# First layer of a four-block transformer step: one norm chain at the end of the feed-forward, the routing's places one key tile later, and VectorE's side work in other portions

## The reference

```python
x = x + attn_a(layernorm(x))   # linear attention: 16 heads of 64, 64 random features, norm, elu feed-forward (512), norm
x = x + ffn(layernorm(x))      # 160 experts, the best 8 by sigmoid score, and a shared expert
x = x + attn_b(layernorm(x))   # softmax attention, causal within 256 tokens
x = x + ffn(layernorm(x))
```

```python
kv = einsum('bnhm,bnhd->bhmd', kf, v); num = einsum('bnhm,bhmd->bnhd', qf, kv)
den = einsum('bnhm,bhm->bnh', qf, sum(kf, axis=1)); attn_out = einsum('bnhd,hdo->bno', num / den, Wo)
out1 = norm(x + attn_out, ln1); h = elu(out1 @ W1 + b1)
return norm(out1 + h @ W2 + b2, ln2)
```

## Time and profile before

| | |
|---|---|
| median of three runs | 2445.37 us |
| profiled execution | 2448.35 us, of which 2445.9 us span |
| TensorE busy | 1809.1 us, 74% |
| VectorE busy | 1664.6 us, 68% |
| GpSimd busy | 1276.6 us, 52% |
| ScalarE busy | 1139.9 us, 47% |
| granted TensorE clock, mean | 0.83 |
| stages 1, 2, 3 with the feed-forward behind them | about 200 to 810 us of the span |

### The profile page before, as it was taken

The page is one execution under the profiler, slowest core; times in us unless marked ns, Lnnn a source line. Parts: engine busy times, 40 slices in busy tenths (PEclk is TensorE's granted clock), DMA queues, the critical chain, the costliest instruction groups (busy, mean ns, idle before and its releaser), DMA issues. The chain is left out here.

```text
span 2445.9 us, 45027 instructions
## 1 busy us (share of the span) xinstructions
PE 1809.1 (74%) x15531; PEld 1047.1 (43%) x15531; DVE 1664.6 (68%) x4684; ACT 1139.9 (47%) x2101; POOL 1276.6 (52%) x1244
## 2 busy tenths in 40 slices
PE   8997787787687678774989888988899868874000
PEld 4555455445445455551334343443344346653000
DVE  8477578588678664576888878888887266376222
ACT  4663553454544356651548554534453536653000
POOL 0162166667756675763436430531342477577776
PEclk9998898789789689995789887988886879987555
DMA  9940101201203687875133221212211378775222
GB/s 358 343 190 30 44 3 57 78 6 43 80 20 143 234 272 246 268 242 129 44 88 78 53 77 36 61 62 47 60 61 42 137 280 285 252 246 183 60 61 55
DMA packets 143465, 309.20 MB, mean 126 GB/s; under 512 B 30668, under 2 KB 45644, under 8 KB 137340
## 3 DMA queue, kind: packets, MB, share of 16 engines
q1 hardware_dynamic: 110472, 239.16, 29.3%
q0 software_dynamic: 32768, 67.17, 9.3%
HBM read 163.12 MB, written 142.70 MB: 125 GB/s over the span
## 5 line engine op out<-in xcount | busy, mean ns | idle before, releaser
L1523 POOL DMA_INDIRECT slots_in<-g_xs,g_place x512 | 519.1, 1014 | 307.5 <-ACT b_pT L2614 155.1
L2614 ACT ACTIVATE b_pT<-b_psE 128x512 f32<-128x512 f32 (+3 forms) x768 | 331.9, 492 | 383.6 <-PE b_psE L2515 206.9
L1550 POOL DMA_INDIRECT r_xs<-slots_out,g_place x336 | 328.1, 976 | 230.2 <-issue 86.0
L2366 DVE TENSOR_REDUCE b_peak<-b_psM 128x1 f32<-128x512 f32 (+3 forms) x768 | 388.9, 549 | 82.8 <-PE b_psM L2498 50.1
L2495 PE MATMUL b_psM<-b_stacks 72*128 72x512 bf16 (+3 forms) x768 | 264.5, 382 | 54.3 <-DVE b_peak L2366 22.1
L2511 PE MATMUL b_psE<-b_stacks 75*128 75x512 bf16 (+3 forms) x768 | 240.8, 369 | 14.1 <-ACT b_pT L2614 12.7
L1550 POOL DMA_INDIRECT g_xs<-slots_out,g_place x176 | 174.3, 990 | 90.0 <-issue 50.6
L2525 PE MATMUL b_psV<-b_pT,b_vb 128*32 128x512 f32 (+3 forms) x1536 | 182.6, 558 | 4.0 <-ACT b_ctxu L2621 3.7
L2495 PEld LDWEIGHTS b_psM<-b_stacks 72*128 72x128 bf16 x768 | 80.3, 106 | 224.3 <-DVE b_peak L2366 124.7
L2131 DVE COPY m_staged_w<-wgd 128x192 f32 x512 | 107.2, 279 | 89.8 <-PE m_psY L1836 81.2
L2131 DVE COPY n_staged_w<-wgd 128x192 f32 x512 | 108.3, 281 | 84.9 <-PE n_psY L1836 76.1
(11 more groups left out here) (658 smaller groups left out, 4016.6 us busy)
## 6 DMA issues: line engine op xcount, KB each, us to landing
wgd<-in_w_gdT SPq DMA_DIRECT2D x20, 1536.0 KB, 10.6
slots_in<-g_xs SPq DMA_DIRECT2D x26, 1024.0 KB
m_rows<-slots_in SPq DMA_DIRECT2D x104, 256.0 KB
slots_out<-m_y SPq DMA_DIRECT2D x104, 256.0 KB
n_rows<-slots_in SPq DMA_DIRECT2D x104, 256.0 KB
slots_out<-n_y SPq DMA_DIRECT2D x104, 256.0 KB
key_dash<-a_dashes SPq DMA_DIRECT2D x32, 512.0 KB, 6.3
a__arg<-key_dash SPq DMA_DIRECT2D x32, 512.0 KB
```

The lines of the kernel that those rows point to most:

```text
L1523: self.nc.gpsimd.indirect_dma_start(self.G.slots_in[self.h], bass.IndirectOffsetOnAxis(self.G.place[:, TPH * self.h + t, k:k + 1], 0), sel ...
L1550: self.nc.gpsimd.indirect_dma_start(self.rows(i)[:, k, :], None, self.G.slots_out[t // TPH], bass.IndirectOffsetOnAxis(self.G.place[:, t, ...
L2366: nc.vector.reduce_max(to, taking()[:, 0:size], AX.X).then_inc(m_taken, 1)
L2614: nc.scalar.activation(pT[:, e % KEPT, h, q0:HALF], psE[:, j % BANKS, q0:HALF], ACT.Exp, scale=SCALE).then_inc(e_taken, 1)
```

## The change

There are five edits. `ffn_finish` is split: `ffn_sums` and `ffn_stats` do the first half's sum and statistics at once, and one chain over all 8 tiles stands in place of two over 4; scalings come for each half, then the gain and the addition for each half. The routing's first seven fills and the sigmoids stand one key tile later, the others half a tile to one tile later. `PIECES` has other numbers for tiles 0 to 4, and the phases in `Q` are moved with the fills. The sends of the query part begin at tile 6, three a tile, in place of tile 5, two a tile. The last feed-forward uses the same split functions.

```diff
@@ -59,8 +59,8 @@
 CHUNKS = 10
 CHUNK = EXPERTS // CHUNKS
 BPH = BATCH // HALVES
-SEND_A_KEY_TILE, SEND_A_QUERY_TILE, SEND_IN_FFN, SEND_IN_ROUTE = 5, 2, 6, 5
-FIRST_SEND = 5
+SEND_A_KEY_TILE, SEND_A_QUERY_TILE, SEND_IN_FFN, SEND_IN_ROUTE = 5, 3, 6, 5
+FIRST_SEND = 6
 SEND_A_STEP = 2
 BESIDE = 12
 DEEP = 4
@@ -786,9 +786,9 @@
     KEPT_Q = 4
     ROOT = float(DN / np.sqrt(2.0))
     p = b - 1 if b else None
-    PIECES = ((3, 2, 5), (5, 2, 5), (3, 1, 3), (3, 1, 3), (2, 2, 4)) + 3 * ((5, 3, 6),)
-    FILLS = ((2, 4), (2, 5), (3, 0), (3, 2), (3, 4), (3, 5), (4, 0), (5, 2), (5, 4), (6, 4), (6, 5), (7, 0), (7, 2))
-    SIGMOIDS = (4, 0)
+    PIECES = ((2, 2, 4), (3, 2, 4), (4, 2, 4), (5, 2, 5), (3, 2, 5)) + 3 * ((5, 3, 6),)
+    FILLS = ((3, 4), (3, 5), (4, 0), (4, 2), (4, 4), (4, 5), (5, 0), (6, 0), (6, 2), (7, 0), (7, 2), (7, 4), (8, 0))
+    SIGMOIDS = (5, 0)
     TURNED, SCORED, HIDDEN, ADDED, COUNTED = range(0, 2), range(2, 5), range(5, 7), range(7, 9), 9
     RANKS = range(10, 13)
     OWNERS_AT = (2, 1)
@@ -813,7 +813,7 @@
         if b:
             Q = Shared()
             Q.LOGITS, Q.RANKS = SCORED[-1] + 1, RANKS[-1] + 1
-            Q.bias, Q.scores, Q.shared, Q.counts = (3, 2), (4, 1), ((5, 1), (5, 2)), (6, 2)
+            Q.bias, Q.scores, Q.shared, Q.counts = (4, 2), (5, 1), ((6, 0), (6, 1)), (7, 0)
 
             def until(phase):
                 while now[0] < phase:
@@ -918,9 +918,9 @@
             pieces = iter(())
             if b:
                 ffn_limits(nc, dve, G, N, p, B)
-                for _ in ffn_finish(nc, dve, G, F, N, p, B, 0):
-                    pass
-                pieces = itertools.chain(ffn_finish(nc, dve, G, F, N, p, B, 1), routed())
+                ffn_sums(nc, dve, G, N, p, B, 0)
+                ffn_stats(nc, G, N, p, 0)
+                pieces = itertools.chain(ffn_finish(nc, dve, G, F, N, p, B), routed())
 
             def side(t, phase, count):
                 now[0] = (t, phase)
@@ -1407,23 +1407,33 @@
                                            ALU.min, ALU.add).then_inc(B.elu_ready, 1)
 
 
-def ffn_finish(nc, dve, G, F, N, b, B, u):
-
-    here, tiles = slice(PER * u, PER * (u + 1)), range(PER * u, PER * (u + 1))
-    rows, y2, stats, mv, rstd, var, half = G.xn[:, b, :, :], B.y2, N.stats, N.mv, N.rstd[:, here], N.var[:, here], N.half[:, here]
+def ffn_sums(nc, dve, G, N, b, B, u):
+
+    here, rows = slice(PER * u, PER * (u + 1)), G.xn[:, b, :, :]
     dve.wait_ge(B.own_ready, u + 1)
     dve.wait_ge(B.down_done, u + 1)
     nc.vector.tensor_tensor(rows[:, here, :], B.own[:, here, :], B.psY[:, u, :].rearrange("p (t d) -> p t d", d=DM), ALU.add).then_inc(B.sums_taken, 1)
     nc.vector.drain()
+
+
+def ffn_stats(nc, G, N, b, u):
+
+    for t in range(PER * u, PER * (u + 1)):
+        nc.vector.bn_stats(N.stats[:, t, :], G.xn[:, b, t, :])
+    nc.vector.drain()
+
+
+def ffn_finish(nc, dve, G, F, N, b, B):
+
+    rows, y2, mv, rstd, var, half = G.xn[:, b, :, :], B.y2, N.mv, N.rstd[:], N.var[:], N.half[:]
+    ffn_sums(nc, dve, G, N, b, B, 1)
     yield
-    for t in tiles:
-        nc.vector.bn_stats(stats[:, t, :], rows[:, t, :])
-    nc.vector.drain()
+    ffn_stats(nc, G, N, b, 1)
     yield
-    for t in tiles:
-        nc.vector.bn_aggr(mv[:, t, :], stats[:, t, :])
-    nc.vector.drain()
-    nc.vector.tensor_scalar(half, mv[:, here, 1], EPS_LN_A, None, ALU.add)
+    for t in range(TPB):
+        nc.vector.bn_aggr(mv[:, t, :], N.stats[:, t, :])
+    nc.vector.drain()
+    nc.vector.tensor_scalar(half, mv[:, :, 1], EPS_LN_A, None, ALU.add)
     nc.vector.drain()
     nc.vector.tensor_scalar(rstd.bitcast(I32), half.bitcast(I32), -0.5, float(0x5F3759DF), ALU.mult, ALU.add)
     nc.vector.tensor_scalar(half, half, -0.5, None, ALU.mult)
@@ -1439,15 +1449,18 @@
         if turn == 1:
             yield
     yield
-    for t in tiles:
-        nc.vector.tensor_scalar(y2[:, t, :], rows[:, t, :], mv[:, t, 0:1], N.rstd[:, t:t + 1], ALU.subtract, ALU.mult)
-    nc.vector.drain()
-    yield
-    nc.vector.tensor_tensor(y2[:, here, :], y2[:, here, :], F.g2[:].unsqueeze(1).to_broadcast([P, PER, DM]), ALU.mult)
-    nc.vector.drain()
+    for u in range(UNITS):
+        for t in range(PER * u, PER * (u + 1)):
+            nc.vector.tensor_scalar(y2[:, t, :], rows[:, t, :], mv[:, t, 0:1], N.rstd[:, t:t + 1], ALU.subtract, ALU.mult)
+        nc.vector.drain()
+        yield
     dve.wait_ge(B.x_ready, 1)
-    nc.vector.tensor_tensor(G.x[:, b, here, :], G.x[:, b, here, :], y2[:, here, :], ALU.add)
-    yield
+    for u in range(UNITS):
+        here = slice(PER * u, PER * (u + 1))
+        nc.vector.tensor_tensor(y2[:, here, :], y2[:, here, :], F.g2[:].unsqueeze(1).to_broadcast([P, PER, DM]), ALU.mult)
+        nc.vector.drain()
+        nc.vector.tensor_tensor(G.x[:, b, here, :], G.x[:, b, here, :], y2[:, here, :], ALU.add)
+        yield
 
 
 def ffn_a(nc, stage, G, F, N, b, send, loads):
@@ -1486,9 +1499,10 @@
         @block.vector
         def _(dve):
             ffn_limits(nc, dve, G, N, b, B)
-            for u in range(UNITS):
-                for _ in ffn_finish(nc, dve, G, F, N, b, B, u):
-                    pass
+            ffn_sums(nc, dve, G, N, b, B, 0)
+            ffn_stats(nc, G, N, b, 0)
+            for _ in ffn_finish(nc, dve, G, F, N, b, B):
+                pass
 
 
 def group_order(lead, first=0):
```

More of the change, by code:

```diff
@@ L1441, in ffn_finish @@
     yield
-    for t in tiles:
-        nc.vector.tensor_scalar(y2[:, t, :], rows[:, t, :], mv[:, t, 0:1], N.rstd[:, t:t + 1], ALU.subtract, ALU.mult)
-    nc.vector.drain()
-    yield
-    nc.vector.tensor_tensor(y2[:, here, :], y2[:, here, :], F.g2[:].unsqueeze(1).to_broadcast([P, PER, DM]), ALU.mult)
-    nc.vector.drain()
-    dve.wait_ge(B.x_ready, 1)
-    nc.vector.tensor_tensor(G.x[:, b, here, :], G.x[:, b, here, :], y2[:, here, :], ALU.add)
-    yield
+    for u in range(UNITS):
[3 more added lines that the diff above has]
+        yield
+    dve.wait_ge(B.x_ready, 1)
+    for u in range(UNITS):
[3 more added lines that the diff above has]
+        nc.vector.tensor_tensor(G.x[:, b, here, :], G.x[:, b, here, :], y2[:, here, :], ALU.add)
+        yield
 def ffn_a(nc, stage, G, F, N, b, send, loads):
```

## The result

| | before | after |
|---|---|---|
| median of 20 runs each, us | 2445.72 | 2458.09 |
| ratio, 95% interval | | 1.0048, [1.0034, 1.0062] |
| profiled execution, span, us | 2445.9 | 2457.5 |
| first sum of the feed-forward at the head of stage 1, 2, 3 and of the last one, us | 217.06, 403.99, 597.20, 789.93 | 218.18, 407.72, 608.20, 808.94 |

The change costs about 12 us. That is inside the stated range, but the sum said +2.5, and the time fell where rival (2) had put it: that the range held is not to the credit of the working. In the profile the first layer is 19 us longer up to the last feed-forward; of that 7 come back in this pair of executions, 0.6 in the last feed-forward and the rest in code that is the same in both, as its waits fall otherwise. So I read places inside a stage, counted from its first feed-forward sum, and trust the medians for the total.

A forecast was written before the change was run, and what follows sets the result against it. No engine is full in the key part, so chains across engines (key tile, routing) bound it; the query part is full on VectorE. Terms -0.1 + 1.5 + 0.8 - 0.1 + 0.4 = +2.5 us gave 2448, range 2433 to 2460.

The forecast's parts named there:

- rival (2): Each stage: VectorE waits 4 to 6 us for ranks, TensorE then idles into the low clock; +10, 2458; chance 0.2.
- First tiles: Stage 2's first key tiles, one norm chain for two: argument 0 comes 0.7 us earlier, argument 1 1.8 earlier.
- Routing's start: Turned rows wait for key tile 3's copies: second turned copies 0.95, 5.6, 4.3 us later in stages 1, 2, 3.
- Picks and ranks: Routing up to the rank copies: picks 2.1, 5.9, 4.6 us later; ranks in use at 306.6, 500.3, 692.5.
- Rival (1): Low clock between the two shared products goes, key(6) under 2.5: 15 us gained in all, 2433; chance 0.2.
- The tail: From ranks in use to the spreading of sums: 14.5, 16.5, 14.4 us; shifts -0.1, +1.5, -0.1 by stage.
- a sign of being right: Later turned copies and picks, VectorE idle before ranks and stage 2's second sum, spread sums within 2 us of old place.
- Behind the spreading: Query tile 3, where VectorE is full, gets one more piece of 0.76 in stage 2: +0.8 us.
- Sends: Query part: six sends in both orders, the last two weighings wait for as many as before: 0.
- my own signs of being wrong: Picks no later, key(6) at 1.9, a wait at the weighings of query tiles 6 and 7, or total below 2440.
- Scalings: Feed-forward scalings in tile 0: put at 0; were all eight held up, +2.6 in stages 2 and 3 each, 2453.
- Last feed-forward: Runs alone; second sum waits for GpSimd until about 797.6, one chain behind it: 807.9 against 807.5, +0.4 us.

The follow-up runs named there:

- kernels 7 and 8: The changed kernel with useless extra matmuls on TensorE before the second query dash, 14 in the first (ratio 1.0045) and 9 in the second (1.0078).
- kernel 4: The changed kernel with the two old norm chains and old sends, leaving the routing's new places and VectorE's pieces for them; ratio to before 1.0056.
- kernel 7: The changed kernel with 14 useless extra matmuls on TensorE between the second query product and the second query dash; ratio to before 1.0045.
- kernel 9: The kernel before, with VectorE's rank work put behind query argument 0 and the copy of keys times values; 2451.07 us, ratio 1.0031.
- kernel 5: The changed kernel with query peak 0, argument 0 and the keys-times-values copy ahead of all but VectorE's first rank piece; 2443.62 us, ratio 1.0009.

## Why the prediction was off, step by step

All places are relative to the stage's first sum.

- **First tiles: right.** The second sum waits 6.40 us for GpSimd (said: 7), argument 1 of stage 2 is 2.4 us earlier (1.8).
- **Routing's start: right in stage 2.** The second turned copies are 3.6, 5.6, 3.3 us later (0.95, 5.6, 4.3). Key(4) takes 2.64 and 3.62 in stages 2 and 3, not 1.9.
- **Picks and ranks: right.** Picks are 1.9, 4.3, 4.5 later (2.1, 5.9, 4.6; the places of the earlier trace rows), with key(6) at the low clock, 3.17 and 3.63; ranks in use 4.1, 6.1, 5.7 later (3.6, 7.0, 5.1). Rival (1), which needed key(6) under 2.5, was out with that.
- **The tail: too short by 5.6.** From ranks in use to the spreading I had 14.5, 16.5, 14.4; it takes 16.3, 17.7, 17.0. I took the operations' durations as they were before. In the new place they run beside GpSimd's folds of query tiles 0 and 1: the addition of line 653 takes 1.86 in stages 1 and 3 and 2.39 in stage 2, where it took 1.49 in each before, and single small operations of the places that start beside such a fold take over 1.2 (1.29 at line 687 in stage 1, 1.25 at 685 in stage 3, where 0.20 is usual). In stages 2 and 3 the slow dash adds 0.4. The spreading is 2.2, 1.8, 3.1 later within its stage, 7.1 in all, where I had said 1.3; in stage 3 it is beyond the 2 us that I had named as a sign of being right.
- **Behind the spreading: the step that failed.** I had 0.8 for one piece; it is 0, 3.9, 2.8, 6.7 in all. I had seen both links, "VectorE idle some 5 us before the first rank operation" and TensorE behind it, and put them aside by the earlier trace rows: the spreading takes 1.98 although TensorE had stood idle some ten microseconds before. But there 7 to 9 us of work lay between the end of the wait and the spreading; the change moves the wait right ahead of the dash. TensorE's wait is also longer than VectorE's wait for the ranks (4.25, 3.08, 4.70 us), since the rank work itself, some 10 us of it, now stands in between. Before, the work just behind the wait was slow too: 3.52 us for the last sums in stage 1 where the ones ahead took 2.05. The Trainium skill, TensorE: Matmul & The Clock Gate, "What's actually happening", has the array fall to 1.2 GHz when idle; stages 2 and 3 agree (0.50 granted from 517 to 532), and kernels 7 and 8, which fill the idle time, show it as the cause of the slow dash. By that rule I had reckoned 2458, which is the measured time; but kernel 4 has the same idle time and not the 3.9 and 2.8 us, so the agreement to the microsecond is luck in part.
- **Sends: 0 said, 1.9 measured.** I had counted the sends and not what stands behind them, a 3.06 us wait, of which all but 0.7 a stage was paid by scalings before. A wait at these weighings was one of my own signs of being wrong, and it came.
- **Scalings.** Those of the feed-forward took 2.31 us for eight in stage 2, so the 2.7 that I had held ready for SBUF — State Buffer, "Who interferes with whom" (the Trainium skill), did not fall due there; eight scalings of the routing's norm (459) took 3.80 at 439.78, where GpSimd ran a fold from 440.68. I had also misread the kernel before: GpSimd was busy beside the scaling of 1.11 as well, with sends (at 421.06), and beside the one of 3.82 it ran an addition from 410.04. In these rows it is the additions and folds that hold a scaling up, and not the sends. VectorE was held up as the page has it, at another operation than the one I had looked at.
- **Last feed-forward:** 0.6 less, +0.4 said. Behind it VectorE waited 2.88 us for the start of the next section before and waits 0.78 now; this gives back 2.1 more, so that the next section's statistics start 16.3 us later than before (826.77 against 810.44).

7.1 + 6.7 + 1.9 - 0.6 = 15.1 us against a sum of 2.5. The rest of the 19 in the profile is feed-forward stretches that are the same in both (26.0 to 28.1 us each over all kernels, by the clock) and 1.1 ahead of stage 1. Less the 2.1 behind the last feed-forward it is 13.0. Between these and the 12.4 of the medians I can't tell, with one profiled execution of the kernel before.

It was rival (2) that happened, in two stages of three: the spreading took over 3 us there. Its price of 10 us was nearly right, but by another sum: it held clock alone, and measured are 6.7 us behind the spreading and 7.1 of a later spreading. The forecast missed it since it asked whether the spreading had been slow, and not what would stand ahead of it.

## What to carry to other kernels

An engine that finishes its part earlier gains nothing until the next engine's list has the operation that it waits for in front: after moving work along one engine, follow each wait to the place where it lands, and reorder that engine too. A wait that is moved takes its low clock with it, onto what now stands right behind it (the dash, in every stage here), and sometimes onto more. And a new wait on a full engine costs only what the stalls that it replaces did not already cost.

## What the hardware showed beside

- The granted clock stood at 0.50 from 517 to 532 in stage 2 and likewise in stage 3, in both executions of the changed kernel, though TensorE had work all the while (dash, one-row spreading, 64-row fold, query(2)); it rose only then. In kernel 7, with no idle time ahead, query(2) still took 3.30 us in stage 2 behind spreading and fold, and in the kernel before, stages 1 and 3, it took 3.78 behind a dash and a spreading at the full clock. So the low clock also comes without a wait close ahead, behind this one-row and 64-row work; not always, for in stages 1 and 2 of kernel 9 query(2) takes 1.99 and 1.98 in the same place.
- A small integer operation on VectorE (0.23 us) took 2.38 us beside a weighing of 2.63 on GpSimd (from 531.28), an addition of 1.49 took 2.88 beside one of 2.35 (from 507.03), both in kernel 5. The first ends just after the weighing, the second 1.35 us after it: the delay is what was left of the other engine's instruction and does not shrink with one's own length.
